# Three-bank exponentials in six halves of the third attention, and a one-bank last tile

## The chip, the cores and the metric

The kernel runs on one core of a Trainium2 chip. The metric is the device time of one execution in microseconds (us); lower is better.

## The reference

The input is `x`, 1024 tokens of 128 features, and a context of 6404 rows of 96 features. Four layers follow one another, each a cross-attention over the context and a feed-forward part, each added to `x`. Layers 0 and 2, the first and the third attention, have 16 heads of 8 features; this is what the change touches:

```python
q = (query @ Wq + bq).reshape(B, Nq, H, D).transpose(0, 2, 1, 3)
k = (key_value @ Wk + bk).reshape(B, Nkv, H, D).transpose(0, 2, 1, 3)
v = (key_value @ Wv + bv).reshape(B, Nkv, H, D).transpose(0, 2, 1, 3)
attn = jnp.einsum('bhqd,bhkd->bhqk', q, k) * scale
...
attn = jax.nn.softmax(attn, axis=-1)
...
x = jnp.einsum('bhqk,bhkd->bqhd', attn, v).reshape(B, Nq, Cq)
return x @ Wo + bo
```

## The kernel before, in words

The keys are cut into `ST` = 51 tiles of 128: `SF` = 50 full ones and a last one with 6404 - 50 x 128 = 4 keys, the rest of which is padding whose values and ones are zero. The 16 heads are `NG` = 4 groups of `G` = 4 heads, the queries two halves of 512. An attention of this kind (`attention8`) is thus 8 passes over the 51 tiles, `gh` = 0 to 7, called halves here.

For one tile of one half:

- POOL stages the tile (`stage_tile`, L1452 to L1458): the keys of the group into `kst` (L1455), 32 rows (a band) for each head, and the values with a column of ones into `vst` (L1456). Both are rings of `RING` = 3 tiles. A tile is staged when the value matmuls of the tile three before are done (`av_done`).
- PE makes the scores (`qk`, L583 to L591): 4 matmuls of one band each, 512 columns, into 4 of 6 PSUM banks (L587). They wait for both staged parts, and for the exponential that last read the banks.
- ACT takes the exponential of two banks at once, 1024 columns (`exps8_loop`, L1203), so two instructions for a tile, into `probs`, a ring of 3 tiles. A hardware loop runs over all 8 halves.
- PE multiplies the four heads' exponentials with the values (`av`, L601), each head into its own 32 partitions of bank 6 or 7, summed up over the 51 tiles. These fp32 matmuls run as two passes each.

PE's order is written out in `straight` (L648 to L686): in each step first the scores of tile t+1 (at the end of a half tile 0 of the next), then a side job, then the values of tile t. After tile 2 of a half come four matmuls with the sums of the half before (L684). The side jobs of the first attention are projections for the second (L482, L488, `PART_AT`: 52 parts in tiles 3 to 50 of every half). Those of the third are: in half 0 keys and values that this attention needs itself (L531, L553), in halves 1, 3 and 5 the keys of the next group (`next_keys`, L531, spread by `V3_AT` over tiles 5 to 48), in half 6 a covariance (L505), in half 7 values of the fourth attention (L520). Their results are copied out of PSUM by DVE (L1836 to L1839 for keys). Halves 2 and 4 have none.

Semaphores: `staged` counts POOL's copies (2 a tile), `scores_ready` and `exp_done` pairs of banks (2 a tile), `av_done` tiles. Each engine takes its instructions in order, so a wait holds up all that stands behind it.

Depending on the data, a mode with subtracted maxima can run instead (`group`, `maxima`, `shift8`); with these inputs the plain one runs.

## Time and profile before

| | |
|---|---|
| median of 3 runs | 3867.96 us (3867.46 to 3876.79) |
| the profiled execution's own time | 3869.18 us |
| its span, first to last instruction | 3867.2 us |
| TensorE clock granted, mean of the span | 0.981 |
| busy: PE, ACT, DVE, POOL | 94%, 66%, 46%, 13% |
| chain that ended last: PE, ACT, issue, DVE | 70%, 12%, 11%, 4% |
| exponentials of the first and third attention, L1203 | 1632, 12% of the chain |

The trace is of one profiled execution. The first attention runs from about 79 to 871 us of the span, the third from 2547 to 3309. Busy time of an engine is a union of its instructions' times, and a matmul's end is modelled; the time from one start to the next says more on rates than a duration.

### The profile page before, as it was taken

What the parts mean: (1) busy time and instruction counts of PE and PEld (TensorE: products, weight loads), DVE (VectorE), ACT (ScalarE), POOL (GpSimd) and SP (SyncE); (2) the same over time, 40 slices, a digit from 0 to 9 for tenths busy, and PEclk for the clock granted to TensorE, in tenths of its full rate; (3) what the DMA queues carried; (4) which work ended last, traced back from release to release, by engine and by line L of the source; (5) the groups of instructions that cost most, each with busy time, mean ns of one, the idle gap of its engine ahead of it and who ended that gap; (6) DMA issues with size and microseconds to landing.
All of it is one profiled execution on the core that took longest, in us unless ns stands there. A gap on an engine that the chain in (4) does not pass through costs nothing.

```text
span 3867.2 us, 86196 instructions
## 1 busy us (share of the span) xinstructions
PE 3650.5 (94%) x32286; PEld 1383.1 (36%) x32290; DVE 1791.0 (46%) x1797; ACT 2565.1 (66%) x2720; POOL 490.9 (13%) x1844
## 2 busy tenths in 40 slices
PE   6999999999989999999999999989888899897989
PEld 4333333334433333333333333332222223453444
DVE  3222222224377777777777777643121211343344
ACT  4999999993445555555555555479999999301321
POOL 1222222220000000000000000023222332001200
PEclk8999999999999999999999999999999999998989
DMA  5323232212111111111111110000000000000000
GB/s 174 102 78 105 83 101 82 97 69 65 56 38 39 38 40 40 40 39 38 39 38 39 43 38 1 1 23 4 4 4 4 4 29 2 20 24 1 0 12 28
DMA packets 104943, 162.72 MB, mean 42 GB/s; under 512 B 23108, under 2 KB 46048, under 8 KB 103104
## 3 DMA queue, kind: packets, MB, share of 16 engines
q1 hardware_dynamic: 104640, 158.16, 12.8%
q8 instruction: 253, 4.15, 0.5%
q14 instruction: 50, 0.41, 0.0%
HBM read 93.24 MB, written 64.88 MB: 41 GB/s over the span
## 4 chain that ended last, share of the span: by engine, by line
PE 70%; ACT 12%; issue 11%; DVE 4%; ACTq 1%; SPq 1%; DMA 1%; POOL 0%; DVEq 0%; POOLq 0%
PE ps L840 18%; PE ps L865 18%; ACT probs L1203 12%; PE ps L601 7%; PE ps L587 4%; PE ps L744 3%; PE ps L482 3%; PE ps L723 2%; PE ps L1012 2%; PE ps L1023 2%; PE ps L488 2%; PE ps L1071 2%; PE ps L1085 1%; PE ps L730 1%; PE ps L277 1%
## 5 line engine op out<-in xcount | busy, mean ns | idle before, releaser
L1203 ACT ACTIVATE probs<-ps 128x1024 f32<-128x1024 f32 x1632 | 1514.2, 1068 | 53.6 <-PE ps L587 53.4
L1301 ACT ACTIVATE probs<-ps 128x1024 f32<-128x1024 f32 x808 | 827.8, 1025 | 593.6 <-PE ps L840 579.4
L2093 DVE TENSOR_TENSOR vbuf<-vbuf,probs 128x1024 f32<-128x1024 f32 x784 | 952.8, 1223 | 329.8 <-ACT probs L1301 329.8
L601 PE MATMUL ps<-probs,vst 128*32 128x512 f32 x6528 | 860.5, 599 | 76.8 <-ACT probs L1203 76.3
L587 PE MATMUL ps<-qz,kst 32*128 32x512 f32 x3264 | 414.0, 495 | 22.2 <-issue 13.5
L587 PEld LDWEIGHTS ps<-qz,kst 32*128 32x128 f32 x3264 | 160.6, 182 | 707.8 <-issue 638.6
L1895 DVE COPY qs<-ps 128x512 f32<-128x512 f32 (+1 forms) x208 | 141.7, 681 | 577.9 <-PE ps L482 280.1
L1455 POOL CAST kst<-kb 128x128 fp32r (+1 forms) x816 | 250.5, 307 | 1228.7 <-PE ps L601 1132.5
L840 PE MATMUL ps<-probs,kb 64*64 64x512 f32 x2560 | 332.2, 589 | 0.0
L840 PE MATMUL ps<-probs,qz 64*64 64x512 f32 x2048 | 268.2, 594 | 6.7 <-issue 6.5
L865 PE MATMUL ps<-probs,qz 64*64 64x512 f32 x2048 | 267.3, 592 | 2.6 <-DVE kb L2118 1.8
L865 PE MATMUL ps<-probs,kb 64*64 64x512 f32 x2048 | 265.8, 589 | 0.0
L601 PEld LDWEIGHTS ps<-probs,vst 128*32 128x32 f32 x6528 | 170.8, 109 | 216.4 <-ACT probs L1203 166.3
L1456 POOL COPY vst<-vbuf 128x36 f32 (+1 forms) x816 | 208.4, 255 | 0.0
L840 PEld LDWEIGHTS ps<-probs,kb 64*64 64x64 f32 x2560 | 97.9, 133 | 176.7 <-issue 176.7
L1536 POOL COPY probs<-kb 128x512 f32<-128x512 f32 x16 | 11.5, 745 | 1129.1 <-PE ps L840 1077.0
L1221 ACT ACTIVATE probs<-ps,stat 128x1024 f32<-128x1024 f32 x51 | 56.8, 1114 | 125.9 <-PE ps L1012 125.9
L840 PE MATMUL ps<-probs,klo 64*64 64x512 f32 x1024 | 132.9, 589 | 0.0
L865 PE MATMUL ps<-probs,klo 64*64 64x512 f32 x1024 | 132.9, 589 | 0.0
L865 PE MATMUL ps<-probs,qs 64*64 64x512 f32 x1024 | 132.9, 589 | 0.0
L840 PEld LDWEIGHTS ps<-probs,qz 64*64 64x64 f32 x2048 | 78.0, 134 | 151.0 <-issue 145.9
L1836 DVE COPY klo<-ps 128x512 f32<-128x512 f32 (+1 forms) x51 | 34.7, 681 | 205.3 <-PE ps L531 205.3
(412 smaller groups left out, 3178.0 us busy)
## 6 DMA issues: line engine op xcount, KB each, us to landing
kv_scratch<-qs SPq DMA_DIRECT2D x192, 256.0 KB, 2.0
kb<-kv_scratch SPq DMA_DIRECT2D x72, 256.0 KB, 2.9
qz<-kv_scratch SPq DMA_DIRECT2D x64, 256.0 KB, 2.9
kb<-k_scratch SPq DMA_DIRECT2D x12, 816.0 KB, 7.0
vbuf<-in_L_ffn_W SPq DMA_DIRECT2D x32, 256.0 KB, 3.0
klo<-kv_scratch SPq DMA_DIRECT2D x32, 256.0 KB, 2.9
k_scratch<-klo SPq DMA_DIRECT2D x12, 512.0 KB, 4.1
qs<-kv_scratch SPq DMA_DIRECT2D x24, 256.0 KB, 3.0
```

Of the source, the lines that this page charges most:

```text
L482: mm = pe.matmul(bank[cut, at:at + k1 - k0], w[0][:, cut], ctxT[:, c0 + k0:c0 + k1], start=True, stop=True)
L587: mm = pe.matmul(ps[:, (4 * r + j) % (2 * RING), :], kst[band, r, :], qh[band, half, :], start=True, stop=True)
L601: mm = pe.matmul(ps[32 * j:32 * j + 32, 6 + half, :], vst[:, r, 32 * j:32 * j + 32], probs[:, r, j * HT:(j + 1) * HT], start=start, stop=stop)
L744: mm = pe.matmul(ps[:, 4 + h, :], wts[:, F + f * D:F + (f + 1) * D], hid[:, f, h, :], start=(f == 0), stop=(f == NF - 1))
L840: mm = pe.matmul(ps[key, 2 * b + e, :], kk[t // 4][head, (t % 4) * P + HD64 * kh:(t % 4) * P + HD64 * (kh + 1)], qp[head, odd, kh if both ...
L865: mm = pe.matmul(ps[head, 4 + 2 * (kh if i == LAST1 else h) + kh, :], vv[t // 4][key, (t % 4) * P + HD64 * e:(t % 4) * P + HD64 * (e + 1)] ...
L1203: act.activation(probs[:, r, b * T:(b + 1) * T].rearrange("p (h n) -> p h n", h=2), ps[:, 2 * buf:2 * buf + 2, :], ACT.Exp, scale=HD8 ** - ...
L1301: act.activation(pr1[:, (u + (u == LAST1) + 2 * odd) % 4], ps[:, 2 * b:2 * b + 2, :], ACT.Exp, scale=HD64 ** -0.5)\
L1455: pool.tensor_copy(kst[:, r, :], keys).then_inc(s["staged"], 1)
L1456: pool.tensor_copy(vst[:, r, :].rearrange("p (j w) -> p j w", j=G)[:, :, 0:HD8 + 1], vbuf[:, bass.ds(t * (H * (HD8 + 1)) + g * (G * (HD8 + ...
L1895: dve.tensor_copy(kvst[:, slot, 0:wd], ps[:, 7 - half, 0:wd]).then_inc(s["kv_moved"], 1)
L2093: dve.tensor_tensor(sum1[:, odd, h], sum1[:, odd, h], e, ALU.add).then_inc(s["added"], 1)
```

## The change

- **Triples.** In halves 1, 2, 3, 4, 5 and 7 of the third attention (`TRIPLES`; its value is the set of banks that the half begins with) scores and exponentials go by three banks: `qk_triple` makes 3 heads' scores into banks 0 to 2 or 3 to 5 in turn, `exps8_triples` takes them in one instruction of 1536 columns. With the one-bank tail a half has 201 banks, 67 triples. Halves 0 and 6 stay with pairs (`by_pairs`). PE's order is in `by_triples`.
- **Tail.** In both attentions the last tile's 4 keys are staged block-diagonally (`stage_tail`, a multiply by `bands`): head j's keys stand in columns 32j to 32j+31 of its band, so that one matmul over all rows gives the four heads' scores in one bank, 32 partitions each. One exponential of 512 columns, and value matmuls of 32 rows and 32 columns.
- **Staging.** In the third attention `kst` of a tile waits for the scores of the tile three before and no longer for its values; scores wait for staged keys alone, the value matmuls for staged values. POOL's loops there are written out.
- **Jobs.** `V3_AT` puts the 26 half jobs into tiles 5 to 44. The mode with maxima, which doesn't run here, does its jobs after the stream.

The diff, cut to its core:

```diff
-V3_AT = [RING + 2 + k * (ST - RING - 3) // V3_PARTS for k in range(V3_PARTS)]
+V3_AT = [RING + 2 + k * (ST - RING - 7) // V3_PARTS for k in range(V3_PARTS)]
...
+TRIPLES = {1: 1, 2: 0, 3: 1, 4: 0, 5: 1, 7: 1}
+LAST3 = (G * SF + 1) // 3 - 1
+
+
+def pairs_after(u):
+    return 2 * ST if u == LAST3 else 3 * (u + 1) // 2
+
...
+                def qk_triple(gh, u):
+                    bank = (TRIPLES[gh] + u) % 2 * 3
+                    heads = [divmod(3 * u + k, G) for k in range(3)]
+                    pe.wait_ge(s["staged"], (gh * ST + heads[-1][0]) * 2 + STAGED[layer] + 1)
+                    if u >= 2:
+                        done = gh * (2 * ST) + pairs_after(u - 2)
+                    elif gh - 1 in TRIPLES:
+                        done = (gh - 1) * (2 * ST) + pairs_after(LAST3 - 1 + u)
+                    else:
+                        done = gh * (2 * ST) - 3 * (1 - u)
+                    pe.wait_ge(s["exp_done"], done + UNITS[layer] + RING)
+                    for k, (t, j) in enumerate(heads):
+                        band = slice(32 * j, 32 * j + 32) if t < SF else slice(0, P)
+                        mm = pe.matmul(ps[:, bank + k, :], kst[band, t % RING, :], qh[band, gh % 2, :], start=True, stop=True)
+                    mm.then_inc(s["scores_ready"], pairs_after(u) - pairs_after(u - 1))
 
...
+                    if n:
+                        pe.wait_ge(s["staged"], (t - TILES[layer]) * 2 + STAGED[layer] + 2)
                     pe.wait_ge(s["exp_done"], (t - TILES[layer]) * 2 + UNITS[layer] + 2 + RING)
...
+                        if stop:
+                            mm = pe.matmul(ps[band, 6 + half, :], vst[band, r, band], probs[band, r, 0:HT], start=start, stop=stop)
+                        else:
+                            mm = pe.matmul(ps[band, 6 + half, :], vst[:, r, band], probs[:, r, j * HT:(j + 1) * HT],
+                                           start=start, stop=stop)
...
+                def begin2(gh, step):
+                    if gh == 2 * NG:
+                        return
+                    if step == 0:
+                        queries_ready(gh // 2, gh % 2)
+                    if gh in TRIPLES:
+                        qk_triple(gh, step)
+                    elif step < 2:
+                        qk_pair(gh, step)
...
+                def by_pairs(gh):
+                    for t in range(ST):
+                        if t + 1 < SF:
+                            qk(gh % 2, gh * ST + t + 1 + TILES[2], (t + 1) % RING)
+                        else:
+                            begin2(gh + 1, t + 1 - SF)
+                        if t + 2 == SF:
+                            qk(gh % 2, gh * ST + SF + TILES[2], SF % RING, True)
+                        values2(gh, t)
...
+                def by_triples(gh):
+                    for i in range(ST // RING):
+                        last = i + 1 == ST // RING
+                        if i or gh - 1 not in TRIPLES:
+                            qk_triple(gh, 4 * i + 2)
+                        if last:
+                            begin2(gh + 1, 0)
+                        else:
+                            qk_triple(gh, 4 * i + 3)
+                        values2(gh, 3 * i)
+                        if last:
+                            begin2(gh + 1, 1)
+                        else:
+                            qk_triple(gh, 4 * i + 4)
+                        values2(gh, 3 * i + 1)
+                        if last:
+                            begin2(gh + 1, 2)
+                        else:
+                            qk_triple(gh, 4 * i + 5)
+                        values2(gh, 3 * i + 2)
+
...
+            def exps8_triples(gh, layer):
+
+                flat = probs[:, :, :].rearrange("p r n -> p (r n)")
+
+                def triple(i, v, last=False):
+
+                    bank = (TRIPLES[gh] + v) % 2 * 3
+                    act.wait_ge(s["av_done"], i * RING + (min(v, RING - 1) + gh * ST + TILES[layer] + 1))
+                    act.wait_ge(s["scores_ready"], i * (2 * RING) + (gh * (2 * ST) + UNITS[layer] + (2 * RING if last else pairs_after(v))))
+                    act.activation(flat[:, v * (3 * HT):(v + 1) * (3 * HT)].rearrange("p (h n) -> p h n", h=3), ps[:, bank:bank + 3, :],
+                                   ACT.Exp, scale=HD8 ** -0.5).then_inc(s["exp_done"], 3 if last else pairs_after(v) - pairs_after(v - 1))
+
+                with act.Fori(0, ST // RING - 1) as i:
+                    for v in range(4):
+                        triple(i, v)
+                for v in range(3):
+                    triple(ST // RING - 1, v, v == 2)
+
+            def exps8_loop(layer, ready, base, triples=()):
...
+                    r = SF % RING
+                    act.wait_ge(s["av_done"], SF + (gh * ST + TILES[layer] + 1))
+                    act.wait_ge(s[ready], gh * (2 * ST) + 2 * ST + base)
+                    act.activation(probs[:, r, 0:HT], ps[:, 4 * r % (2 * RING), :], ACT.Exp, scale=HD8 ** -0.5)\
+                        .then_inc(s["exp_done"], 2)
...
             def stage_tile(layer, gh, t, r, par, g, keys):
 
-                pool.wait_ge(s["av_done"], gh * ST + t + TILES[layer] + 1)
-                pool.tensor_copy(kst[:, r, :], keys).then_inc(s["staged"], 1)
+                if layer == 2 and gh * ST + t >= RING:
+                    pool.wait_ge(s["scores_ready"], (gh * ST + t) * 2 + (UNITS[layer] - 2 * RING + 2))
+                    pool.tensor_copy(kst[:, r, :], keys).then_inc(s["staged"], 1)
+                    pool.wait_ge(s["av_done"], gh * ST + t + TILES[layer] + 1)
+                else:
+                    pool.wait_ge(s["av_done"], gh * ST + t + TILES[layer] + 1)
+                    pool.tensor_copy(kst[:, r, :], keys).then_inc(s["staged"], 1)
+                values(t, r, g)
+
+            def stage_tail(layer, gh, par, g):
+
+                r = SF % RING
+                pool.wait_ge(s["scores_ready"], (gh * ST + SF) * 2 + (UNITS[layer] - 2 * RING + 2))
+                ins = pool.tensor_tensor(kst[:, r, :].rearrange("p (j k) -> p j k", j=G),
+                                         kb[:, par, SF * P:SF * P + 32].unsqueeze(1).to_broadcast([P, G, 32]),
+                                         bands[:, :].unsqueeze(2).to_broadcast([P, G, 32]), ALU.mult)
+                ins.then_inc(s["staged"], 1)
+                pool.wait_ge(s["av_done"], gh * ST + SF + TILES[layer] + 1)
+                values(SF, r, g)
+
```

How the order moves PE's instructions in the third attention, in a half with jobs (half 3; `L587` and `L618` are scores, `L531` is a half job for the next keys, `L601` and `L636` are values; a row's x is the number of matmuls). Before:

```order
L587 MATMUL ps<-qz,kst 128x512 x4
L531 MATMUL ps<-ctxT,w64 32x256 x4
L601 MATMUL ps<-probs,vst 32x512 x4
L587 MATMUL ps<-qz,kst 128x512 x4
L601 MATMUL ps<-probs,vst 32x512 x4
L587 MATMUL ps<-qz,kst 128x512 x4
L531 MATMUL ps<-ctxT,w64 32x256 x4
L601 MATMUL ps<-probs,vst 32x512 x4
```

And of the change:

```order
L618 MATMUL ps<-qz,kst 128x512 x6
L531 MATMUL ps<-ctxT,w64 32x256 x4
L636 MATMUL ps<-probs,vst 32x512 x4
L618 MATMUL ps<-qz,kst 128x512 x3
L636 MATMUL ps<-probs,vst 32x512 x4
L618 MATMUL ps<-qz,kst 128x512 x3
L531 MATMUL ps<-ctxT,w64 32x256 x4
L636 MATMUL ps<-probs,vst 32x512 x4
L618 MATMUL ps<-qz,kst 128x512 x6
L531 MATMUL ps<-ctxT,w64 32x256 x4
```

The scores of three tiles were three groups of 4 matmuls, one ahead of each tile's values; now they are four groups of 3, two of which stand side by side (x6).

PE at the turn from half 2 to half 3, before (third row: the scores of half 3's tile 0):

```order
L587 MATMUL ps<-qz,kst 128x512 x4
L601 MATMUL ps<-probs,vst 32x512 x4
L587 MATMUL ps<-qz,kst 128x512 x4
L601 MATMUL ps<-probs,vst 32x512 x4
L587 MATMUL ps<-qz,kst 128x512 x4
L601 MATMUL ps<-probs,vst 32x512 x4
L587 MATMUL ps<-qz,kst 128x512 x4
```

And of the change (`L634` are the values of the last tile, 50):

```order
L618 MATMUL ps<-qz,kst 128x512 x3
L636 MATMUL ps<-probs,vst 32x512 x4
L618 MATMUL ps<-qz,kst 128x512 x6
L636 MATMUL ps<-probs,vst 32x512 x4
L618 MATMUL ps<-qz,kst 128x512 x3
L636 MATMUL ps<-probs,vst 32x512 x4
L618 MATMUL ps<-qz,kst 128x512 x3
L634 MATMUL ps<-probs,vst 32x512 x4
L618 MATMUL ps<-qz,kst 128x512 x3
L636 MATMUL ps<-probs,vst 32x512 x4
```

Before, one group of the next half's scores stood ahead of the last tile's values. Now the x6 row holds the last triple of half 2 and triple 0 of half 3; the x3 rows behind the values of tiles 48 and 49 are triples 1 and 2 of half 3, ahead of the values of tiles 49 and 50.

POOL at a turn, of the change, behind the branch around the mode that doesn't run (`L1590` stages keys, `L1610` values; tiles 0, 1 and 2 of the next half):

```order
L1658 UNCONDITIONAL_BRANCH
L1590 COPY kst<-kb 128x128 [waits scores_ready,v_copied,k_split]
L1610 COPY vst<-vbuf 128x4x9 [waits av_done]
L1590 COPY kst<-kb 128x128 [waits scores_ready]
L1610 COPY vst<-vbuf 128x4x9 [waits av_done]
L1590 COPY kst<-kb 128x128 [waits scores_ready]
L1610 COPY vst<-vbuf 128x4x9 [waits av_done]
```

A tile's keys and values are in one queue: keys of tile 1 stand behind the values of tile 0, which wait for value matmuls.

## Rows read from the trace of the kernel before

**Rows 1.** The page: span, busy time by engine, costliest groups (line, engine, op | busy, mean | idle before).

```profile
span 3867.2 us, 86196 instructions
PE 3650.5 (94%) x32286; PEld 1383.1 (36%) x32290; DVE 1791.0 (46%) x1797; ACT 2565.1 (66%) x2720; POOL 490.9 (13%) x1844
...
L1203 ACT ACTIVATE probs<-ps 128x1024 f32<-128x1024 f32 x1632 | 1514.2, 1068 | 53.6 <-PE ps L587 53.4
...
L601 PE MATMUL ps<-probs,vst 128*32 128x512 f32 x6528 | 860.5, 599 | 76.8 <-ACT probs L1203 76.3
L587 PE MATMUL ps<-qz,kst 32*128 32x512 f32 x3264 | 414.0, 495 | 22.2 <-issue 13.5
```

**Rows 2.** Timeline of ACT, third attention: start, length, instructions [idle before, releaser].

```profile
2654.12 93.61 ACT L1203 ACTIVATE probs<-ps 128x1024 f32<-128x1024 f32 x102 [0.61 <-PE ps L587]
2748.34 93.60 ACT L1203 ACTIVATE probs<-ps 128x1024 f32<-128x1024 f32 x102 [0.61 <-PE ps L587]
...
3221.29 86.27 ACT L1203 ACTIVATE probs<-ps 128x1024 f32<-128x1024 f32 x94 [0.62 <-PE ps L587]
```

**Rows 3.** Windows: stretch, us, then busy PE, PEld, DVE, ACT, POOL, clock, DMA.

```profile
core 0: us, PE busy (x) PEld busy (x) DVE busy (x) ACT busy (x) POOL busy (x), PEclk, DMA share, GB/s
2655.00:2748.00 93.00, 85.80 (x824) 23.50 (x820) 29.07 (x43) 92.73 (x102) 30.86 (x102) 1.00 0.02 4
2749.00:2842.00 93.00, 76.64 (x612) 18.32 (x608) 4.40 (x3) 92.95 (x102) 23.43 (x102) 1.00 0.01 4
485.00:584.00 99.00, 96.38 (x1247) 36.06 (x1244) 22.82 (x31) 95.47 (x102) 23.75 (x102) 1.00 0.32 98
```

**Rows 4.** Timeline of PE, third attention, tiles with a job.

```profile
2898.73 0.50 PE L587 MATMUL ps<-qz,kst 32*128 32x512 f32 x4
2899.16 0.64 PE L531 MATMUL ps<-ctxT,w 128*32 128x256 f32 x8
2899.62 1.04 PE L601 MATMUL ps<-probs,vst 128*32 128x512 f32 x8
2900.59 0.51 PE L587 MATMUL ps<-qz,kst 32*128 32x512 f32 x4
```

**Rows 5.** Timeline of PE, third attention, half 2, no jobs.

```profile
2801.67 1.06 PE L601 MATMUL ps<-probs,vst 128*32 128x512 f32 x8 [0.32 <-ACT probs L1203]
2802.68 0.50 PE L587 MATMUL ps<-qz,kst 32*128 32x512 f32 x4
2803.50 1.06 PE L601 MATMUL ps<-probs,vst 128*32 128x512 f32 x8 [0.33 <-ACT probs L1203]
```

**Rows 6.** First attention at a turn: timeline of PE, then of ACT.

```profile
573.37 0.51 PE L587 MATMUL ps<-qz,kst 32*128 32x512 f32 x4
573.80 0.43 PE L488 MATMUL ps<-w,ctxT 128*32 128x128 f32 x8
574.04 1.06 PE L601 MATMUL ps<-probs,vst 128*32 128x512 f32 x8
575.08 0.51 PE L587 MATMUL ps<-qz,kst 32*128 32x512 f32 x4
575.99 1.07 PE L601 MATMUL ps<-probs,vst 128*32 128x512 f32 x8 [0.41 <-ACT probs L1203]
...
581.96 1.94 ACT L1203 ACTIVATE probs<-ps 128x1024 f32<-128x1024 f32 x2 [0.61 <-PE ps L587]
680.67 1.94 ACT L1203 ACTIVATE probs<-ps 128x1024 f32<-128x1024 f32 x2 [0.61 <-PE ps L587]
```

**Rows 7.** Groups of ACT by shape: isolated activations of one and two banks.

```profile
L1240 ACT ACTIVATE work<-ps 128x512 f32<-128x512 f32 x32 | 19.0, 595 | 157.7 <-PE ps L730 157.7
L1376 ACT ACTIVATE work<-ps 128x1024 f32<-128x1024 f32 x17 | 17.4, 1024 | 104.4 <-DVE work L2348 77.6 <-PE ps L1071 26.8
```

**Rows 8.** Timeline of POOL: a staged tile of half 2, then one of half 1 beside DVE.

```profile
2802.96 0.30 POOL L1455 CAST kst<-kb 128x128 fp32r x1 [1.37 <-PE ps L601]
2803.20 0.22 POOL L1456 COPY vst<-vbuf 128x36 f32 x1
...
2681.57 0.76 POOL L1456 COPY vst<-vbuf 128x36 f32 x1
```

**Rows 9.** Third attention: PE early in half 0, POOL early in half 6.

```profile
2558.16 0.51 PE L587 MATMUL ps<-qz,kst 32*128 32x512 f32 x4 [1.24 <-POOL vst L1456]
...
3131.86 1.84 POOL L1456 COPY vst<-vbuf 128x36 f32 x1
3133.64 1.82 POOL L1455 CAST kst<-kb 128x128 fp32r x1
```

More of the change, by code:

```diff
@@ L64 @@
 JOBS = 2 * NC
-JSTEPS = (ST - RING) // 2
-JOBS_AT = [[c for c in range(NC) if c * JSTEPS // NC == step] for step in range(JSTEPS)]
 COV_FROM = 16
@@ L687, in attention8, with straight2 @@
+                def straight2():
+                    queries_ready(0, 0)
+                    qk(0, TILES[2], 0)
+                    for gh in range(2 * NG):
+                        if gh in TRIPLES:
+                            by_triples(gh)
+                        else:
+                            by_pairs(gh)
                 if n == 0:
@@ L1465, in stage0 @@
                 mode = mode_of(pool, 0)
-                with pool.Fori(0, NG // 2) as gi:
+                for gi in range(NG // 2):
                     for par in range(2):
@@ L1925, in without_jobs8 @@
                         maxima(layer, p, G, 2 * ST, HUGE)
[L1926 to L1928 removed]
+                        shifts8(p)
                     if p == 1:
```

259 lines of the change are left out of this document (151 added, 108 removed).

## The prediction

> **What bounds the kernel now.** I read the page first: in the whole span PE is busy 94% and ACT 66%, and the exponentials of the first and third attention (L1203) are the costliest ACT group, the value and score matmuls (L601, L587) the ones beside it [rows 1]. The change touches those two stages. "Half h" below is one of the 8 passes (4 groups of heads, 2 halves of the queries) of an attention, h from 0 to 7.
>
> Then the timeline of ACT in the third attention: 102 exponentials without a gap in 93.6 us, a gap of 0.61, and again; from one half to the next 94.22 us [rows 2]. That is 0.918 us for one exponential of 1024 columns, and ACT is busy 92.7 to 93.0 us of 93 [rows 3]. PE is at 76.6 us in a half without side jobs and at 85.8 in one with them [rows 3]: ACT sets the time and PE has room, but not much. PE's timeline gives the pieces, start to start: a group of score matmuls (4 bands at once) 0.43 us, half a side job 0.46, the value matmuls 0.97 [rows 4]; without a job PE stands 0.32 before each tile's values, waiting for ACT, and a tile takes 1.83 [rows 5].
>
> The first attention is another case. PE has a job in nearly every tile, 0.43 + 0.46 + 0.97 = 1.86 us against 2 x 0.918 = 1.84 of ACT, PE busy 96.4 of 99 us, a half 98.7 us long [rows 3, 6]. PE sets the time there.
>
> **A triple on ACT.** No three-bank exponential is in the trace. Isolated activations of PSUM take 595 ns for 512 columns and 1024 ns for 1024 [rows 7]: 0.838 ns a column, so 512 columns more are 0.429 us, and a triple is 0.918 + 0.429 = 1.347, against 1.5 x 0.918 = 1.377 now. The gain per triple is only 0.03 us. The bounds are 1.377 (the cost stays as it is per bank) and 1536 x 0.838 = 1.287 (no fixed part at all); I take 1.347, which is one fixed part, as the exponentials of now have. The one-bank tail is 0.918 - 0.429 = 0.49.
>
> **Halves 2 and 4 (triples, no jobs).** 201 banks of scores are 67 triples: 67 x 1.347 = 90.2, with the 0.6 gap at the previous sums [rows 2] 90.8 against 94.2: -3.4 each, **-6.8**. PE's cycle of three tiles is 4 groups of scores instead of 3 (a triple occupies the array as long as four bands do, since the columns set the time) and 3 values: 4 x 0.43 + 3 x 0.97 = 4.63 against 4 x 1.347 = 5.39 of ACT. It fits.
>
> **Halves 1, 3, 5, 7 (triples, jobs).** Now 26 half jobs lie in the 40 tiles 5 to 44. A tile with a job costs PE 4.63/3 + 0.46 = 2.00 us, one without 1.54; ACT needs 1.80 for either. PE has become the slower one where a job stands. If all of the lead is carried over, the 40 tiles take PE's 40 x 1.54 + 26 x 0.46 = 73.7; if none is, 26 x 2.00 + 14 x 1.80 = 77.1. The other 11 tiles are 41 banks or 13.7 triples, 18.4 us, and the gap 0.6. So a half takes between 92.7 and 96.1. Only two sets of three banks exist, hence one triple of lead at most; I take the middle, 94.6, which is 0.4 more than now: **+1.6** for four. The Trainium skill (Perfetto Trace Analysis, Optimizing Scalar/DVE Operations) advises larger ScalarE operations where the engine is saturated, and smaller ones where it isn't and holds up others. By the first part these halves would gain like halves 2 and 4, -13.6 in place of +1.6; by the second they lose up to 1.9 each, +7.6. ACT is saturated before the change and, by the rows' sum, no longer after it.
>
> **The four turns from triples to triples** (1-2, 2-3, 3-4, 4-5). The second fragment of the order shows scores of the next half standing between the last value matmuls. Triple 1 of the next half needs keys of its tile 1. POOL stages key and value tiles in one queue, and the values of its tile 0 wait for the values' matmuls of tile 48. From rows: value matmuls start, 1.29 us later POOL's copy starts, 0.24 later the next, which lasts 0.30 [rows 5, 8]: keys 1.83 after the start of tile 48's values. PE is there after 0.97, stands 0.86, and the value matmuls of tile 49 stand behind it in PE's queue; triple 2 does the same behind tile 49. With the tail's scores, which need all rows of the array and can't lie beside the bands of their triple (0.43 more), that is 2 x 0.86 + 0.43 = 2.15 of PE. The bounds are 0 (ACT's lead covers it) and 2.15; ACT has but one triple of lead, and I take 1.9, little below the upper bound because POOL's code there loses its loop instructions: **+7.6**.
>
> **Halves 0 and 6 (pairs).** The tail saves ACT 2 x 0.918 - 0.49 = 1.35. Half 0 is bound by PE as the first attention is, so that gives nothing, but scores no longer wait for staged values, which cost 1.24 us once at its start [rows 9]. In half 6 POOL's copies of 1.8 us cost about as much, beside the centring of the context on DVE [rows 9]; the keys get past part of it. I take -1 for each: **-2**. Bounds: +0.4 and -1.35 - 1.2.
>
> **First attention.** Eight tails save ACT 1.35 each, PE nothing: one group of scores and two passes of values as before. At its turn PE goes on without idling through the next half's first scores, the job and the values of tile 50, and first waits for ACT in the tile after that [rows 6]; that wait is for exponentials that couldn't start before the new scores. I take **0**, and -1.35 x 8 = -10.8 as the bound. The Trainium skill (TensorEngine Tiling (Array Packing), Key Properties) says that changing the tiling mode drains TensorE, which speaks against the tail's full-array scores and 32x32 values. The rows bound such a change: values to scores take 0.97, where two passes are 2 x 0.43 = 0.86, so 0.11. The tail's scores stand where the mode changed before too; one or two more per half, 16 halves, are at most +3.5, in the range.
>
> **Rest.** Three constants, four small memsets instead of one, twice, and 4 matmuls for 1: **+0.6**, bounded by 0 and 2.
>
> **Sum**: -6.8 + 1.6 + 7.6 - 2 + 0 + 0.6 = +1.0 us. The profiled execution took 3869.18 us, so 3870.2 there; the median of the three runs is 1.2 lower, 3869.0. A measurement of this kernel can tell about 0.3% (11.6 us) from no change.
>
> **Rivals.**
> - *PE's order costs nothing* (faster, 0.27). Leads carry over, the turns are covered: job halves at 92.7 (-1.5 x 4), halves 2 and 4 -3.4 each, tails in halves 0 and 6 -1.35 each: -15.5, 3852.5. If PE never binds, six halves give -3.4: with the pairs -23, 3845; the first attention's bound on top -10.8, 3834. For it: PE idles 16 us in a half without jobs [rows 3]. Against: PE's sum per tile with a job is above ACT's.
> - *Staging becomes the bound in the halves with jobs* (slower, 0.20). Beside DVE's work for the next keys POOL's value copy takes 0.76 instead of 0.22 [rows 8]. The key tile of the next tile but one is then ready 1.29 + 0.76 + 0.30 = 2.35 us after the value matmuls that free it, and PE asks for it after 0.97 + 0.43 + 0.97 = 2.37: just in time. If the latencies are a little longer, each of 13 chunks costs up to 0.54 in halves 1, 3 and 5, 21 us; with half of that (10.5), no lead carried over (+1.9 x 4 instead of +1.6) and full turns (8.6): -6.8 + 7.6 + 8.6 - 2 + 0.6 + 10.5 = +18.5, 3886.5. It decides from a delay of about 0.15 us per chunk. Against it: key tiles now start with the scores' release and not with the values'.
> - *A triple isn't shorter per bank* (1.377; 0.13): the change then saves ACT nothing outside the tails. Halves 2 and 4 take 67 x 1.377 + 0.6 = 92.9 (-1.3 instead of -3.4, +4.2 for both), the others about 0.7 more each: +7 on the sum, +8, 3876, still within 0.3%.
>
> **How the numbers follow.** The sum above has 0.40, the third rival 0.13: both within 0.3%, 0.53. The first rival gives faster 0.27, the second slower 0.20. The range leaves out about a tenth at either end: it reaches past the first rival's 3852.5 half way to the case in which PE never binds, and to the second's 3886: 3848 to 3886.
>
> **What the profile after would show.** ACT in the third attention: triples 1.35 us apart in halves 2 and 4, a half there 90.8 us plus a turn; with jobs 94 to 96. ACT, gap-free now, should show idle time released by the score matmuls in the job halves; PE should wait for POOL's key copies at the four turns, twice each, by 0.8 to 0.9 us. First attention: halves 98.7 as now. I am wrong if the job halves fall below 92.7 or rise above 96.1, if triples are further apart than 1.38 without a wait, or if the first attention moves by more than 4 us.

## The result, and the profile after

The changed kernel took 3877.68 us (median of 20 runs, 3870.48 to 3885.93), the kernel before 3870.32 on the same chips (median of 20, 3865.84 to 3878.39): ratio 1.0017, 95% interval 1.001 to 1.0024, that is 6.6 us slower (3.9 to 9.3). It counts as no change by the bound of 0.3% and lies inside the forecast range; the forecast was +1.0 us on the sum.

The page of the changed kernel, to be laid beside [rows 1]:

```profile
span 3875.4 us, 84692 instructions
PE 3686.8 (95%) x32248; PEld 1411.5 (36%) x32248; DVE 1794.6 (46%) x1797; ACT 2540.8 (66%) x2500; POOL 468.3 (12%) x1853
...
PE 85%; ACT 6%; DVE 4%; issue 3%; SPq 1%; DMA 0%; POOL 0%; ACTq 0%; DVEq 0%; POOLq 0%
...
L1312 ACT ACTIVATE probs<-ps 128x1024 f32<-128x1024 f32 x1000 | 934.8, 1030 | 54.8 <-PE ps L591 54.4
L1298 ACT ACTIVATE probs<-ps 128x1536 f32<-128x1536 f32 x402 | 550.1, 1521 | 27.4 <-PE ps L618 20.2
L618 PE MATMUL ps<-qz,kst 32*128 32x512 f32 x1206 | 200.5, 494 | 38.0 <-ACT probs L1298 24.3
```

L1298 are the triples' exponentials, L618 their scores, L1312 the pairs' exponentials, L591 the pairs' scores, L636 the value matmuls. ACT is busy 24 us less than before, PE 36 us more. The chain of waits has moved from ACT (12%, now 6%) to PE (70%, now 85%). The lines L618 and L1298 wait for each other: ACT stood 27.4 us before the triples' exponentials, 20.2 of them for their scores, and PE 38.0 before those scores, 24.3 of them for exponentials. Two engines in a ring that both idle are what this document is about.

Half by half, from one copy of the accumulators by DVE to the next, in us (halves of the third attention, and the stage as a whole from ACT's table load to its next one):

| profiled execution | 1 | 2 | 3 | 4 | 5 | 6 | 7 | stage |
|---|---|---|---|---|---|---|---|---|
| before | 94.29 | 94.15 | 94.29 | 94.15 | 94.29 | 95.99 | 94.22 | 764.28 |
| after | 98.29 | 92.48 | 97.90 | 92.48 | 96.11 | 97.82 | 96.41 | 772.74 |
| e1_short_jobs | 93.03 | 93.30 | 93.00 | 92.49 | 90.87 | 95.46 | 96.17 | 756.18 |
| e2_tail_only | 94.44 | 94.21 | 94.47 | 94.20 | 94.47 | 94.65 | 94.05 | 760.49 |
| e3_triples_2_4 | 95.39 | 91.12 | 94.97 | 91.14 | 94.06 | 94.66 | 94.04 | 756.76 |
| e4_jobs_placed | 96.64 | 92.49 | 96.21 | 92.49 | 94.69 | 95.46 | 94.77 | 764.22 |
| e5_keys_ahead | 97.34 | 91.52 | 96.93 | 91.52 | 96.17 | 97.02 | 96.22 | 768.77 |
| e6_jobs_and_keys | 95.68 | 91.53 | 95.28 | 91.53 | 94.69 | 95.45 | 94.77 | 761.02 |
| e7_two_late_tail | 94.48 | 91.16 | 94.08 | 91.16 | 94.06 | 94.67 | 94.05 | 755.40 |
| e8_triples_2_4_6 | 94.49 | 91.15 | 94.08 | 91.14 | 94.10 | 97.51 | 93.66 | 757.50 |

The last PE matmuls of a half stand before its copy, so a turn from half h to h+1 is counted in h. The third attention is 8.46 us longer after the change. The first attention, from table load to table load, is 3.4 us shorter (803.13 against 806.52). 1.7 of that are single longer halves (before 99.22, 99.89 and 98.71 against 98.48 in the others, after 98.83 and 98.78); such halves come and go from trace to trace. The stretch between the two attentions is 5.5 us longer. The change touches next to nothing there, but the granted clock differed: between 1020 and 1060 us it was 0.79 after and 0.91 before, which is 17 us at the lower level against 7. All the rest is 2.4 us shorter. These make the 8.2 us by which the two spans differ.

### The profile page after: what moved, and what is told of

It reads as the page before. It is cut to its first block, busy times and chain, and to the rows that moved or that the text cites. A ratio compares the mean times of both kernels' runs of the same rounds, so it can differ in the third digit from the quotient of the medians.

```text
span 3875.4 us, 84692 instructions
## 1 busy us (share of the span) xinstructions
PE 3686.8 (95%) x32248; PEld 1411.5 (36%) x32248; DVE 1794.6 (46%) x1797; ACT 2540.8 (66%) x2500; POOL 468.3 (12%) x1853
## 4 chain that ended last, share of the span: by engine, by line
PE 85%; ACT 6%; DVE 4%; issue 3%; SPq 1%; DMA 0%; POOL 0%; ACTq 0%; DVEq 0%; POOLq 0%
PE ps L933 18%; PE ps L958 18%; PE ps L636 15%; PE ps L591 5%; PE ps L618 4%; PE ps L488 3%; PE ps L837 3%; PE ps L482 3%; ACT probs L1298 3%; PE ps L816 2%; PE ps L1105 2%; PE ps L1116 2%; ACT probs L1312 2%; PE ps L1164 2%; PE ps L531 1%
## 5 line engine op out<-in xcount | busy, mean ns | idle before, releaser
L1429 ACT ACTIVATE probs<-ps 128x1024 f32<-128x1024 f32 x808 | 827.4, 1024 | 593.8 <-PE ps L933 579.7
L1312 ACT ACTIVATE probs<-ps 128x1024 f32<-128x1024 f32 x1000 | 934.8, 1030 | 54.8 <-PE ps L591 54.4
L636 PE MATMUL ps<-probs,vst 128*32 128x512 f32 x6400 | 844.2, 599 | 15.1 <-ACT probs L1312 13.5
L1298 ACT ACTIVATE probs<-ps 128x1536 f32<-128x1536 f32 x402 | 550.1, 1521 | 27.4 <-PE ps L618 20.2
L591 PE MATMUL ps<-qz,kst 32*128 32x512 f32 x1996 | 253.9, 498 | 18.4 <-issue 13.8
L1610 POOL COPY vst<-vbuf 128x36 f32 (+1 forms) x816 | 189.9, 233 | 572.1 <-PE ps L636 561.8
L591 PEld LDWEIGHTS ps<-qz,kst 32*128 32x128 f32 x1996 | 96.9, 182 | 437.5 <-issue 406.9
L618 PE MATMUL ps<-qz,kst 32*128 32x512 f32 x1206 | 200.5, 494 | 38.0 <-ACT probs L1298 24.3
L636 PEld LDWEIGHTS ps<-probs,vst 128*32 128x32 f32 x6400 | 175.1, 109 | 132.1 <-issue 30.6
L1594 POOL CAST kst<-kb 128x128 fp32r (+1 forms) x403 | 120.8, 300 | 678.6 <-PE ps L636 585.0
L618 PEld LDWEIGHTS ps<-qz,kst 32*128 32x128 f32 x1206 | 80.7, 182 | 321.7 <-issue 168.2
L958 PE MATMUL ps<-probs,klo 64*64 64x512 f32 x1024 | 132.9, 589 | 0.0
```

The costliest lines, as they stand in the source:

```text
L591: mm = pe.matmul(ps[:, (4 * r + j) % (2 * RING), :], kst[band, r, :], qh[band, half, :], start=True, stop=True)
L618: mm = pe.matmul(ps[:, bank + k, :], kst[band, t % RING, :], qh[band, gh % 2, :], start=True, stop=True)
L636: mm = pe.matmul(ps[band, 6 + half, :], vst[:, r, band], probs[:, r, j * HT:(j + 1) * HT], start=start, stop=stop)
L958: mm = pe.matmul(ps[head, 4 + 2 * (kh if i == LAST1 else h) + kh, :], vv[t // 4][key, (t % 4) * P + HD64 * e:(t % 4) * P + HD64 * (e + 1)] ...
L1298: act.activation(flat[:, v * (3 * HT):(v + 1) * (3 * HT)].rearrange("p (h n) -> p h n", h=3), ps[:, bank:bank + 3, :], ACT.Exp, scale=HD8 ...
L1312: act.activation(probs[:, r, b * T:(b + 1) * T].rearrange("p (h n) -> p h n", h=2), ps[:, 2 * buf:2 * buf + 2, :], ACT.Exp, scale=HD8 ** - ...
```

## Where ACT's time went

Windows of the changed kernel, to be laid beside [rows 3]: job half 1, half 2, a half of the first attention.

```profile
core 0: us, PE busy (x) PEld busy (x) DVE busy (x) ACT busy (x) POOL busy (x), PEclk, DMA share, GB/s
2648.00:2744.00 96.00, 91.28 (x817) 28.12 (x814) 30.81 (x43) 91.04 (x67) 24.76 (x101) 1.00 0.01 4
2748.00:2838.00 90.00, 80.05 (x606) 21.03 (x603) 4.74 (x3) 88.58 (x66) 22.25 (x98) 1.00 0.01 2
485.00:584.00 99.00, 96.93 (x1245) 36.19 (x1249) 23.17 (x31) 94.49 (x102) 23.81 (x102) 1.00 0.32 98
```

In half 2 ACT is nearly full; in half 1 ACT stands 5 of 96 us, and PE stands almost as long. Before, ACT was full in both. Now one period of three tiles and four triples in that job half, on PE and then on ACT (start, length, instructions, idle before and releaser):

```profile
2682.11 0.84 PE L618 MATMUL ps<-qz,kst 32*128 32x512 f32 x6
2682.88 1.07 PE L636 MATMUL ps<-probs,vst 128*32 128x512 f32 x8
2684.26 0.51 PE L618 MATMUL ps<-qz,kst 32*128 32x512 f32 x3 [0.31 <-POOL vst L1610]
2684.69 0.64 PE L531 MATMUL ps<-ctxT,w 128*32 128x256 f32 x8
2685.15 1.04 PE L636 MATMUL ps<-probs,vst 128*32 128x512 f32 x8
2686.12 0.50 PE L618 MATMUL ps<-qz,kst 32*128 32x512 f32 x3
2686.55 0.64 PE L531 MATMUL ps<-ctxT,w 128*32 128x256 f32 x8
2687.01 1.04 PE L636 MATMUL ps<-probs,vst 128*32 128x512 f32 x8
```

```profile
2682.67 5.52 ACT L1298 ACTIVATE probs<-ps 128x1536 f32<-128x1536 f32 x4 [0.36 <-PE ps L618]
2688.53 4.14 ACT L1298 ACTIVATE probs<-ps 128x1536 f32<-128x1536 f32 x3 [0.34 <-PE ps L618]
```

The period is 5.86 us on ACT. PE's own work in it is 5.55 (four score groups of 0.43, three values of 0.97, two half jobs of 0.46), and four triples at the 1.34 us at which they start back to back are 5.35. So neither engine fills the period: PE stands 0.31 before the scores at 2684.26, ACT 0.34 to 0.36 once. The scores wait for a triple that ACT began late, and it began late since its own scores had stood behind values and a job on PE. A wait for an exponential costs a fixed time on top, 0.14 us from ACT's end to the start of the scores that it lets go. Scores, exponential and the next scores into the same three banks take 0.55 + 1.45 + 0.14 = 2.14 us; PE's work between the two score groups is 0.43 + 0.43 + 0.97 = 1.83 in two gaps of the four. In such a period the ring, and not a sum, sets the time.

The row at 2684.26 names POOL's value copy as the last to end before these scores. That is a coincidence: in half 5 PE stood over 0.12 us before scores 12 times between 3036 and 3112 us, and each time it started 0.14 us after the end of an exponential. In e5 below POOL's copies stand elsewhere in its queue, and half 5 keeps its time.

What the triples do to the sums is plain, too. Six exponentials of two banks are 6 x 0.918 = 5.51 us of ACT for three tiles, four triples 5.35, so ACT saves 0.16. PE pays a fourth score group, 0.43: with two jobs its sum was 5.12, below ACT's, and is now 5.55, above both. With jobs the triples could gain nothing even without the ring.

The turn from half 2 to half 3, on PE, POOL and ACT:

```profile
2833.24 1.06 PE L636 MATMUL ps<-probs,vst 128*32 128x512 f32 x8
2834.91 0.50 PE L618 MATMUL ps<-qz,kst 32*128 32x512 f32 x3 [0.60 <-POOL kst L1590]
2835.34 1.06 PE L636 MATMUL ps<-probs,vst 128*32 128x512 f32 x8
2837.01 0.51 PE L618 MATMUL ps<-qz,kst 32*128 32x512 f32 x3 [0.60 <-POOL kst L1590]
```

```profile
2834.41 0.22 POOL L1610 COPY vst<-vbuf 128x36 f32<-128x36 f32 x1 [1.94 <-PE ps L636]
2834.56 0.29 POOL L1590 CAST kst<-kb 128x128 fp32r<-128x128 f32 x1
```

```profile
2834.45 1.45 ACT L1298 ACTIVATE probs<-ps 128x1536 f32<-128x1536 f32 x1 [0.24 <-PE ps L636]
2836.61 1.45 ACT L1298 ACTIVATE probs<-ps 128x1536 f32<-128x1536 f32 x1 [0.70 <-PE ps L636]
2838.65 2.79 ACT L1298 ACTIVATE probs<-ps 128x1536 f32<-128x1536 f32 x2 [0.59 <-PE ps L634]
```

This is the wait that the forecast named, twice, released by POOL's key copy that stands behind a value copy. The value copy began 1.17 us after the value matmuls, the keys 0.15 later, so the scores go 1.67 after them, not 1.83. PE stands 0.60 by the row, 0.70 if counted from start to start as the forecast's 0.86 was.

## The experiments

All times below are compared with the kernel before, run on the same chip in between.

**e1_short_jobs.** The edit, in `next_keys` (L531); it leaves out most of the keys' projection for groups 1 to 3, and DVE scales down what is left (L1993):

```diff
-                        mm = pe.matmul(ps[cut, bank, p0:p1], w64[:, g, cut], ctxT[:, c0 + p0:c0 + p1], start=True, stop=True)
+                        q1 = min(p0 + 32, p1) if g else p1
+                        mm = pe.matmul(ps[cut, bank, p0:q1], w64[:, g, cut], ctxT[:, c0 + p0:c0 + q1], start=True, stop=True)
```

> Halves 1, 3 and 5 keep their 26 half jobs, their waits and DVE's copies, but each job's matmuls take 32 columns instead of 256, so the next keys are wrong (DVE scales the rest of the bank down). Theory A, PE is the slower engine in the job halves and loses about 1.5 us more by standing before score triples: with the jobs' PE time gone halves 1 and 3 fall from 98.3 and 97.9 us to 92.5 (as halves 2 and 4), half 5 from 96.1 to about 90.7, the kernel 15 us faster than the changed one. Theory B, POOL's copies beside DVE's work hold PE up: DVE's work stays, so these halves stay above 96 us. Half 7 is untouched, 96.4 or less.

Measured: 3866.34 us in one run (before 3870.35, median of 29). The third attention is 16.6 us shorter than in the changed kernel (15 us were expected in the time). Halves 1, 3 and 5 fell by 5.3, 4.9 and 5.2 us, half 7, whose jobs stayed, by 0.2. (Half 2 has a fall of the clock in it, 93.30 us against 92.49 in half 4.) The same 60 us of half 5, after and in this run (columns as in [rows 3]):

```profile
3033.00:3093.00 60.00, 57.22 (x526) 17.98 (x518) 22.67 (x30) 57.01 (x43) 15.61 (x62) 1.00 0.01 1
```

```profile
3033.00:3093.00 60.00, 54.85 (x576) 15.19 (x567) 21.91 (x33) 60.00 (x46) 16.82 (x66) 1.00 0.01 2
```

ACT is full again, with DVE's and POOL's work as it was (22 us of DVE either way). PE's time in the jobs is the cause; POOL's copies beside DVE are not. The rival of staging in the job halves falls.

**e2_tail_only.** No triples at all, the one-bank tail and the new staging kept:

```diff
-TRIPLES = {1: 1, 2: 0, 3: 1, 4: 0, 5: 1, 7: 1}
+TRIPLES = {}
```

with the next half's tile 0 then asked for at tile 50, as in the first attention.

> No triples: all 8 halves of the third attention by pairs, with the one-bank tail, keys staged early and jobs in tiles 5 to 44. Theory A (the triples cost what the change lost): every half is 94.1 us, 0.1 less than before, half 6 about 95 to 96; against the kernel before -2 to -5 us in all with the first attention's part. If tail and staging are to blame instead, halves stay above 95 and the kernel is slower than before.

Measured: 3867.34 us (median of 12), ratio 0.9989 (0.998 to 0.9998), about 4 us faster than before. In the third attention it is half 6, 95.99 to 94.65, and half 0 with its start, 104.06 to 101.73. Of half 0 less is sure: e3, e7 and e8 have the same code there and took 103.10 to 103.47. Halves 1 to 5 did not gain (+0.05 to +0.2), though each has 1.3 us less of exponentials (two of 0.92 for one of 0.5). The trace shows what takes this, ACT at the turn from half 2 to half 3:

```profile
2837.56 7.44 ACT L1321 ACTIVATE probs<-ps 128x1024 f32<-128x1024 f32 x8 [1.17 <-PE ps L591]
```

The next half's first scores stand in PE's queue behind the values of tile 49. Before, ACT had two exponentials of 0.92 to fill the time until they came; now it has the short one alone, and stands 1.17 us. The tail's gain is handed back in the same place.

**e3_triples_2_4.** As e2, and triples where there are no jobs:

```diff
-TRIPLES = {1: 1, 2: 0, 3: 1, 4: 0, 5: 1, 7: 1}
+TRIPLES = {2: 1, 4: 1}
```

> Triples in halves 2 and 4 alone, where PE has no jobs; the others by pairs. Theory A: halves 2 and 4 take about 91.0 us (no turn from triples to triples is left), halves 1, 3, 5 and 7 94 to 95, in all 5 us less than the tail alone and 13 us less than the changed kernel, 8 us faster than before. If a triple gains nothing per bank, no different from the tail alone.

Measured: 3862.32 us (3853.51 to 3868.53), ratio 0.998 (0.997 to 0.9989), faster than both kernels. Halves 2 and 4 take 91.13, 3.0 less than before; but 1 and 3 rose to 95.39 and 94.97, where e2 has 94.45. The gain of the triples is in these two halves alone, and entering costs 0.5 to 1 us in the half before.

**e4_jobs_placed.** The changed kernel, with the 26 half jobs at fixed places of the period of three tiles. Between the scores into a set of banks and the next into it, PE has only 1.83 us of work in two gaps of the four (ahead of the values of tiles 0 and 2 of the period), and would stand 0.31 there. A job in such a gap fills the wait first. In the other two gaps (2.80 us) there is no wait to fill, so tile 1 gets no job.

```diff
-V3_AT = [RING + 2 + k * (ST - RING - 7) // V3_PARTS for k in range(V3_PARTS)]
+V3_AT = sorted([t for t in range(6, 46, 3)] + [t for t in range(8, 42, 3)])
```

> As the changed kernel, but the 26 half jobs stand in tiles 6, 9, ... 45 and 8, 11, ... 41: in the two of every three tiles where the next triple's scores wait for an exponential that started only 1.83 us of PE's work earlier. Theory A (round trip from scores to exponential to scores, 0.55 + 1.45 + 0.14 = 2.14 us, stands open where no job fills it): job halves 1.1 to 1.4 us shorter each, 4 to 5 us in all. Theory C, PE's plain sum bounds them and the place of a job doesn't matter: within 0.3 us of now. Theory B: no shorter, or longer, since chunks follow one another closer.

Measured: 3870.53 us, ratio 1.0002 (0.9993 to 1.0012), so in the time the whole loss of the change is gone. Each job half is 1.4 to 1.7 us shorter (1.1 to 1.4 expected), and nothing was removed: the same jobs, the same 5.55 us of PE a period. Only where they stand in the ring changed. The score groups that begin three periods in half 1 of this run:

```profile
2679.70 0.85 PE L619 MATMUL ps<-qz,kst 32*128 32x512 f32 x6
2685.19 0.50 PE L619 MATMUL ps<-qz,kst 32*128 32x512 f32 x3
2685.88 0.50 PE L619 MATMUL ps<-qz,kst 32*128 32x512 f32 x3 [0.18 <-POOL vst L1611]
2691.02 0.85 PE L619 MATMUL ps<-qz,kst 32*128 32x512 f32 x6
```

A period of 5.49 us, which is PE's work alone, and one of 5.83 take turns, 5.66 in the mean. The changed kernel's half 5 has both kinds of place: its six periods with a job in tile 1 take 5.87 to 5.93, its six with both jobs in the short gaps 5.49 to 5.93, 5.71 in the mean. Six times 0.24 (5.90 to 5.66) is the 1.4 us that half 5 gained. So the two short gaps are not closed for good: in every second period PE still waits for an exponential (again 0.14 us from its end), now at the second group of the six. Why the periods take turns was not tried. A limit by sums alone gives the same time for either place.

**e5_keys_ahead.** The changed kernel, with POOL's list in another order (`values` is the copy of L1610; the thresholds on `staged` follow it):

```diff
-                            if t < SF:
-                                stage_tile(2, gh, t, t % RING, par, g, kb[:, par, t * P:(t + 1) * P])
+                            stage_key(gh, t, par, g)
...
+                def later_values(t, gh, g):
+                    if pending:
+                        pt, pgh, pg = pending.pop()
+                        pool.wait_ge(s["av_done"], pgh * ST + pt + TILES[2] + 1)
+                        values(pt, pt % RING, pg)
+                    if t is not None:
+                        pending.append((t, gh, g))
```

`stage_key` copies the keys behind their own wait and then calls `later_values`, which copies the values of the tile before.

> The changed kernel, with GpSimd's list in the third attention in another order: the keys of tile g+1 are copied ahead of the values of tile g (each behind its own wait), so that a key copy no longer stands behind a value copy that waits for the value matmuls three tiles back. Nothing else is moved. In the changed kernel's turn from half 2 to half 3 TensorE stood 0.603 us twice before score triples, released by GpSimd's key copy, and the exponentials 1.63 us in all. Theory A (the turns between two halves of triples are set by the queue of GpSimd): these two waits vanish, ScalarE's idle time at a turn falls from 1.6 to 0.6 us or less, and each of the four turns (1 to 2, 2 to 3, 3 to 4, 4 to 5) is 1.0 to 1.5 us shorter: third attention 772.7 to about 768, time 4 to 6 us under the changed kernel's, about 3872. Theory B (the turn is set by the round trip between the two engines, and the key copy only ends last): another releaser takes over with a wait of the same length, the halves move by under 0.3 us each, time within 1.5 us of the changed kernel's. In the job halves away from the turns both theories expect no change (under 0.3 us a half).

Measured: 3875.63 us, ratio 1.0021 (1.0012 to 1.003). By the times no gain can be told. The trace can tell: halves 1 to 4 are each 0.95 to 0.97 us shorter, halves 5 and 7 move by 0.1 and 0.2. PE at the same turn, and ACT:

```profile
2832.59 0.50 PE L625 MATMUL ps<-qz,kst 32*128 32x512 f32 x3 [0.19 <-ACT probs L1306]
2833.02 1.06 PE L642 MATMUL ps<-probs,vst 32*32 32x512 f32 x8
2834.20 0.50 PE L625 MATMUL ps<-qz,kst 32*128 32x512 f32 x3
```

```profile
2832.60 1.45 ACT L1306 ACTIVATE probs<-ps 128x1536 f32<-128x1536 f32 x1 [0.16 <-PE ps L644]
2834.23 5.48 ACT L1306 ACTIVATE probs<-ps 128x1536 f32<-128x1536 f32 x4 [0.17 <-PE ps L642]
```

The two waits of 0.60 are 0.19 or less, ACT's idle time at the turn 0.56 instead of 1.53 (0.24 + 0.70 + 0.59). Theory A holds for what lies at the turns, with 1.0 us where 1.0 to 1.5 were expected. Against it stands half 0, which grew by 0.8 us (104.30 against 103.49; by 0.6 from e4 to e6); why was not tried, and e1, with the changed kernel's code there, took 104.10. The expected 4 to 6 us in the time were not seen: 3.8 less 0.8 is 3, no more than the interval.

**e6_jobs_and_keys.** Both edits together.

> The changed kernel with both edits, the jobs at fixed places of the period of three tiles (which took 1.4 to 1.7 us from each job half and 7 us from the time) and the keys ahead of the values in GpSimd's list. If the two losses are separate, the gains add: 7 + 4 to 6 = 11 to 13 us under the changed kernel's time, third attention near 760, time near 3866, which is still not below the kernel with the block-diagonal tile and halves 2 and 4 alone (3862). If the two are one loss seen twice (ScalarE's lead over TensorE, which either edit restores), it comes out within 1.5 us of the jobs placed alone, 3870.

Measured: 3866.16 us, ratio 0.9996 (0.9987 to 1.0005), 0.0021 or 8 us under the changed kernel's ratio (11 to 13 expected), 0.0006 or 2 us under the jobs placed alone. Halves 1 to 4 fell by 0.93 to 0.96 us from e4, just as they had without the placed jobs; 5 to 7 stood still. The losses are two, and they add. Even so, job halves by triples (94.69 and 94.77, without a turn) don't beat pairs (94.05 to 94.47).

**e7_two_late_tail.** As e3, with the tail's scores one tile later:

```diff
                         else:
+                            if t + 1 == SF:
+                                qk(gh % 2, gh * ST + SF + TILES[2], SF % RING, True)
                             begin2(gh + 1, t + 1 - SF)
-                        if t + 2 == SF:
-                            qk(gh % 2, gh * ST + SF + TILES[2], SF % RING, True)
```

> Triples in halves 2 and 4 alone (the best so far, ratio 0.998 to the kernel before), and in the halves of pairs ahead of them (1 and 3) the scores of the last tile are moved behind the value matmuls of tile 48, directly ahead of the first score triple of the next half. In the run without this edit halves 1 and 3 took 95.39 and 94.97 us where the same halves with pairs behind them took 94.44 and 94.47. Theory A (the 0.7 us comes from the order of PE at the end of these halves: the tail's scores stand ahead of value matmuls whose exponentials then start late): halves 1 and 3 fall to 94.4 to 94.6, third attention from 756.8 to 755, time 1 to 2 us lower, about 3861. Theory B (it is the price of entering a half of triples, whose first triple waits for the last pairs' banks): halves 1 and 3 stay at 95.0 or above, or halves 2 and 4 grow by what 1 and 3 lose; time unchanged within 0.5 us.

Measured: 3861.68 us, ratio 0.9975 (0.9964 to 0.9987). Halves 1 and 3 are 94.48 and 94.08, 0.9 less, and 2 and 4 grew by only 0.03. Theory A is right. PE at the end of half 1, in e3 and then in e7:

```profile
2739.15 0.48 PE L586 MATMUL ps<-qz,kst 128*128 128x512 f32 x1 [1.27 <-ACT probs L1321]
2739.56 1.07 PE L636 MATMUL ps<-probs,vst 128*32 128x512 f32 x8
```

```profile
2736.39 1.06 PE L636 MATMUL ps<-probs,vst 128*32 128x512 f32 x8 [0.35 <-POOL kst L1599]
2737.39 0.49 PE L586 MATMUL ps<-qz,kst 128*128 128x512 f32 x1
2737.81 0.50 PE L618 MATMUL ps<-qz,kst 32*128 32x512 f32 x3
```

One score group too early waited 1.27 us for its bank, with value matmuls behind it that were ready. The difference of e7 to e3 in the times is within the intervals; the two halves show it.

**e8_triples_2_4_6.** Half 6 by triples too:

```diff
-TRIPLES = {2: 1, 4: 1}
+TRIPLES = {2: 1, 4: 1, 6: 1}
```

> Halves 2, 4 and 6 by triples, with the late tail before each. Half 6 lies between the job halves and the halves without jobs: it has a covariance group of 0.13 us on TensorE about once a tile. By pairs it took 94.67 us (two of 0.43 and 0.97 us of TensorE's work a tile, plus these, against 1.81 us of exponentials a tile). Theory A (a half pays by triples as long as TensorE's chain from scores through values and the jobs between them, with the time to and from ScalarE, stays under four triples of 1.34 us a period, 5.35 us): with a covariance in each gap the round trip is 2.14 + 0 us against 1.83 + 0.13 us, still covered, so half 6 goes to 91.2 to 93.0, gains 1.7 to 3.5 us, while half 5 stays at 94.1 and half 7 falls by up to 0.4: third attention 752 to 754, time 2 to 3 us under the kernel with halves 2 and 4, about 3859. Theory B (any work on TensorE between the triples breaks the pace, as in the job halves, and GpSimd's copies in half 6, up to 1.9 us each there, stand behind the waits): half 6 at 94 us or more, no gain, time 3861 to 3864.

Measured: 3861.94 us, ratio 0.9972 (0.9962 to 0.9983), the same as e7. Half 6 took 97.51 us: theory B. PE and POOL in its first tiles:

```profile
3129.93 0.51 PE L618 MATMUL ps<-qz,kst 32*128 32x512 f32 x3 [1.39 <-POOL kst L1599]
3131.88 0.69 PE L618 MATMUL ps<-qz,kst 32*128 32x512 f32 x3 [0.44 <-POOL kst L1599]
```

```profile
3127.96 1.92 POOL L1599 CAST kst<-kb 128x128 fp32r<-128x128 f32 x1
3129.83 1.74 POOL L1619 COPY vst<-vbuf 128x36 f32<-128x36 f32 x1
```

POOL's slow copies [rows 9] now stop PE, and three triples there start 2.20 to 2.53 us apart instead of 1.34, 3.1 us in all. A fall of the clock followed them and is in these spacings too. In the covariance part the four triples of a period take 5.48 to 5.79 us instead of 5.35, another 3.0 us: 91.15 (half 2), 3.1 and 3.0 are 97.3. Score groups there:

```profile
3164.56 0.51 PE L618 MATMUL ps<-qz,kst 32*128 32x512 f32 x3
3166.32 0.50 PE L618 MATMUL ps<-qz,kst 32*128 32x512 f32 x3
3167.90 0.50 PE L618 MATMUL ps<-qz,kst 32*128 32x512 f32 x3
```

From scores over values to scores PE takes 1.40 us without a covariance (0.43 + 0.97), here 1.76 with two and 1.58 with one, so one costs 0.175 and not 0.13. There are one and a half a tile (51 in tiles 16 to 48), not one. That makes 4.63 + 4.6 x 0.175 = 5.44 us of PE a period, above ACT's 5.35, where the expectation looked only at the round trip and called it covered. By half 6 alone the change should cost 2.8 us; the times of e7 and e8 can't be told apart. Half 7 fell by 0.4 as expected.

## Why the prediction was right or wrong

By the terms of the sum (+1.0 us), against the profiled executions (third attention alone: forecast +0.4, measured +8.5):

- **Halves 2 and 4: -6.8 forecast, -6.0 measured** (e3: 91.13 against 94.15, without turns). The triple was right: 1.33 to 1.37 us apart, 1.3385 in the mean, 1.347 forecast. The third rival, 1.377 per triple, is out. The 0.3 us a half that is missing was not taken apart.
- **The four turns: +7.6 forecast, about +6.7 measured.** Halves 2 and 4 are 1.35 longer than in e3, halves 1 and 3 2.2 and 1.8 longer than half 5. The mechanism was the right one: the same wait, twice a turn, by the same copy; e5 took 1.0 us of each away by moving that copy. The rest of a turn, 0.4 to 1.2 us, is left over by subtraction; that it is the tail and the ring itself is not shown.
- **Job halves 1, 3, 5, 7: +1.6 forecast, +7.6 measured. This is the step that failed.** I took 94.6 us as the middle between a lead (scores made ahead of the exponentials) that is carried over (92.7) and none (96.1); the middle is 94.4, and the term should have read +0.8. Half 5, without a turn, has 96.11, half 7 96.41 (96.17 in e1, without a fall of the clock): the end where nothing is carried over, and just past the 96.1 that I had named as the sign of being wrong. The picture was wrong too. My upper bound let PE or ACT be full in each tile, which gives a period with two jobs 2 x 2.00 + 1.80 = 5.80 us wherever they stand. The trace has 5.49 to 5.93 by their place, and that their mean is 5.80 is luck; with a place chosen for each job (e4) the same sum of work takes 94.69. What I had not priced is the ring, the wait for the exponential that frees a set of three banks. These 6.0 us are most of what lies between forecast and result.
- **Half 6: -1 forecast.** The value came out as 97.82, +1.8, but 2.4 us of that are a fall of the clock, below. In e4 and e6, with the same order and no fall, it is 95.46, -0.5. **Half 0:** -1 forecast, -0.6 measured, in a half that differs by 0.4 to 1.4 us between traces with the same code. Behind the last copy the stage ends 1.1 us earlier; with that the terms add up to the 8.5.
- **First attention: 0 forecast.** Its halves take 98.47 to 98.50 before and after, but for a few that are longer in either trace, and the last one takes 0.56 less. The whole stage took 3.4 us less, short of the 4 us that I had named as a limit, about half of it by those longer halves. The **rest** (+0.6) can't be told beside the 5.5 us of the stretch between the two attentions.
- **The sum.** The time lies inside the range, but +6.6 us (+8.2 in the traces) is not +1.0: the job halves came 6.0 us and half 6 2.8 above their terms, the stretch between the two attentions, which has no term but the rest, 5.5; the first attention came 3.4 below. That the total stayed so near zero owes something to luck.
- **Rivals.** "PE's order costs nothing" is refuted by e4, e5 and e7, in each of which only an order was changed. "Staging becomes the bound" is refuted for the job halves by e1, but it is true for half 6 by triples (e8), where POOL's copies are longer still.
- **The skill's rule.** The Trainium skill (Perfetto Trace Analysis, Optimizing Scalar/DVE Operations) has larger operations for a saturated ScalarE and smaller ones where it isn't saturated and holds up others. Its two halves were worth -13.6 and up to +7.6 us here; the job halves gave +7.6. The trace agrees with the second half there (ACT busy 91.04 us of 96, PE waiting for it), and with the first in halves 2 and 4.

What decided whether a half gained was first PE's sum with the fourth score group: 4.63 us a period in halves 2 and 4, below ACT's 5.35, but 5.55 with two jobs and 5.44 with the covariances of half 6 (e8), above it. Only the first two gained. What decided how much the others lost was, besides, whether the trip from a score group over its exponential to the next scores in the same banks fits into PE's work between them: it added 0.25 us to PE's 5.55 in the mean of the periods with two jobs in the changed kernel's half 5, 0.11 with the jobs placed. With two sets of three banks where pairs had three sets of two, an exponential 0.43 us longer has one set of lead less. That the number of sets matters was argued from the code, and not tried by itself: the 8 banks are all in use.

## What to carry to other kernels

Before two engines are joined by larger operations with fewer buffers, write down both engines' sums for a period, with what the new cut adds to the other engine (here 0.16 us saved on ACT and 0.43 added on PE). Then write down the round trip (work, other engine's operation, wait to start again) for each place of the period and lay it beside the first engine's work there; sums per period are a lower bound only. Where an engine's order is written by hand, put side work where the round trip leaves room, and put nothing that waits for a late buffer ahead of work that is ready: two such edits were worth 7 us in all and 0.9 us a half here. Use the larger operation only in the stages where the other engine's sum stays below it, and test the parts of a bundle alone: the half of this change that helps was hidden by the half that doesn't.

## What the runs showed of the hardware

**A wait of 1.3 us on PE was followed by half the clock, in some runs.** At the turn from half 6 to half 7 of the changed kernel PE stood 1.26 us before the tail's scores. PE there, and windows around it:

```profile
3215.85 0.47 PE L586 MATMUL ps<-qz,kst 128*128 128x512 f32 x1 [1.26 <-ACT probs L1312]
3217.56 0.80 PE L618 MATMUL ps<-qz,kst 32*128 32x512 f32 x3
3218.29 1.94 PE L636 MATMUL ps<-probs,vst 128*32 128x512 f32 x8
```

```profile
3213.00:3217.00 4.00, 2.73 (x33) 0.87 (x28) 0.25 (x1) 4.00 (x5) 0.51 (x2) 1.00 0.00 0
3217.00:3221.00 4.00, 4.00 (x26) 0.90 (x22) 0.00 (x0) 1.56 (x2) 0.90 (x4) 0.56 0.00 0
```

PE was busy 2.73 of 4 us, and then the granted clock fell to the lower level (1.2 GHz of 2.4) for 6.8 us; scores took 0.80 instead of 0.50, values 1.94 instead of 1.06, and ACT stood 1.29, 1.20 and 1.08 us. It cost 2.4 us, by the 95.46 of e4. The same wait stands at the same turn in e1, e4, e5 and e6 (1.25 to 1.27 us, PE busy 2.74 of 4 us around it in e1 and e5). In e5 the clock fell behind it as well (0.84 and 0.73 granted in the two stretches of 4 us from 3208, which is 3.4 us at the lower level), and half 6 took 97.02; in e1, e4 and e6 it did not, and half 6 took 95.45 or 95.46. What made the difference is not shown. In e8 the fall came behind POOL's stalls (1.39 and 0.44 us), in e1 at the turn from half 2 to half 3 behind two waits of 0.60 (0.65 granted from 2834 to 2838 us). So a short stall can be paid twice.

**Matmuls behind two waits started 0.09 us later than behind one.** The times here are from the end of an exponential to the start of the matmuls that it let go, in the third attention from 2655 to 3120 us. Before, the values of a tile waited for `exp_done` alone and started 0.053 us after the end (165 times); at the start of a half they waited for another semaphore as well, and it was 0.144 (5 times), as for the scores, which always wait for `staged` too. With the change the values there wait for `staged` in every tile, and in e2 all 164 took 0.143 or 0.144. In the first attention, whose values kept their one wait, it stayed at 0.053 after the change, and at 0.144 only at the start of a half. So it goes with the second wait and not with the kind of matmul, though the other semaphore had been raised before. The ring's 2.14 us hold 0.14 of this; whether 0.09 of it can be saved was not tried.

**POOL's copies** of 0.22 to 0.30 us took up to 1.92 us in the first tiles of half 6 in each of the four traces read there (before, after, e7, e8); before, PE stood 1.33 and 0.44 us for them, in e2 no wait there is over 0.42, as the staging of keys no longer waits for values (half 6 95.99 before, 94.65 in e2).
